# Graph attention on one core: weight loads on ScalarE's queue, residual rows in eight loads, other places for two steps, and a new order of the last two tiles

## The reference

```python
n, d = x.shape                      # 2048, 256
h = Wq.shape[1] // d                # 8
q = (x @ Wq).reshape(h, n, d)
k = (x @ Wk).reshape(h, n, d)
v = (x @ Wv).reshape(h, n, d)
a = jnp.einsum('hnd,hmd->hnm', q, k) * d ** (-0.5)
a = a + adj + adj
mask = adj == 0.0
a = jnp.where(mask, -1000000.0, a)
a = jax.nn.softmax(a, axis=-1)
a = jnp.where(mask, 0.0, a)
out = jnp.einsum('hnm,hmd->hnd', a, v)
out = out.transpose(1, 0, 2).reshape(n, h * d)
x = layernorm(x + out @ Wout)       # over the last axis, eps 1e-05
```

## Time and profile before

| | |
|---|---|
| median of 3 runs | 1853.81 us (1853.4 to 1855.88) |
| the profiled execution | 1851.97 us |
| its span in the trace | 1850.2 us |
| TensorE busy (matmul) | 1808.3 us, 98% |
| VectorE, ScalarE, GpSimd busy | 1117.0, 851.5, 983.8 us |
| moved by the 16 DMA engines | 345.96 MB, 187 GB/s on average |

### The profile page before, as it was taken

The page is one execution under the profiler, slowest core; times in us unless marked ns, Lnnn a source line. Parts: engine busy times, 40 slices in busy tenths (PEclk is TensorE's granted clock), DMA queues, the critical chain, the costliest instruction groups (busy, mean ns, idle before and its releaser), DMA issues.

```text
span 1850.2 us, 29363 instructions
## 1 busy us (share of the span) xinstructions
PE 1808.3 (98%) x10272; PEld 1580.0 (85%) x10272; DVE 1117.0 (60%) x2316; ACT 851.5 (46%) x1411; POOL 983.8 (53%) x764
## 2 busy tenths in 40 slices
PE   7989899999999999999999999999999999999997
PEld 6978788888898888988889888888888888898886
DVE  6788855555555555555655555555555556556667
ACT  4645554344554444544454444544454444554442
POOL 6787765444644446444564445634455444544443
PEclk9999999999999999999999999999999999999999
DMA  7787765666656666566664666656665566655664
GB/s 229 226 283 238 249 211 156 177 191 186 195 147 187 191 195 182 150 185 186 199 187 143 194 185 190 181 157 194 189 187 168 160 197 196 189 166 155 180 180 116
DMA packets 186962, 345.96 MB, mean 187 GB/s; under 512 B 39360, under 2 KB 96704, under 8 KB 170432
## 3 DMA queue, kind: packets, MB, share of 16 engines
q1 hardware_dynamic: 146112, 193.06, 37.2%
q10 hardware_dynamic: 40704, 151.03, 25.5%
HBM read 190.84 MB, written 18.87 MB: 113 GB/s over the span
## 4 chain that ended last, share of the span: by engine, by line
PE 87%; DVE 3%; issue 1%; SPq 1%; DMA 0%; POOL 0%; ACT 0%; DVEq 0%; ACTq 0%
PE bank L409 34%; PE y_bank L432 22%; PE bank L374 17%; PE y_bank L430 12%; PE y_bank L428 1%; SPq L306 1%; DVE blocks L653 1%; DVE zero_mark L691 0%; DVE y_acc L743 0%; POOL p_split L480 0%; DVE t_p L630 0%; DVE m_sb L697 0%; DMA raw_x<-in_x_dram 0%; PE bank L394 0%; ACT m_sb L560 0%
## 5 line engine op out<-in xcount | busy, mean ns | idle before, releaser
L480 POOL TENSOR_TENSOR p_split<-p_turned,p_split 128x512 fp32r<-128x512 f32 x512 | 651.5, 1301 | 628.7 <-ACT p_split L541 628.1
L409 PE MATMUL bank<-k_split,q_split 128*128 128x512 f32 x3072 | 790.0, 392 | 0.0
L432 PE MATMUL y_bank<-v_split,p_split 128*128 128x512 f32 x1920 | 701.8, 399 | 0.0
L409 PEld LDWEIGHTS bank<-k_split,q_split 128*128 128x128 f32 x3072 | 577.4, 188 | 110.5 <-issue 0.3
L630 DVE CUSTOM_DVE_ANT_0 t_p<-bank,m_sb 128x512 f32<-128x512 f32 x512 | 351.2, 687 | 339.9 <-PE bank L409 317.5
L430 PE MATMUL y_bank<-v_split,p_split 128*128 128x256 f32 x2048 | 555.7, 282 | 0.0
L532 ACT ACTIVATE t_p<-t_p,small 128x2048 f32<-128x2048 f32 x128 | 256.8, 2006 | 442.3 <-DVE small L642 442.3
L432 PEld LDWEIGHTS y_bank<-v_split,p_split 128*128 128x128 f32 x1920 | 362.7, 189 | 76.1
L430 PEld LDWEIGHTS y_bank<-v_split,p_split 128*128 128x128 f32 x2048 | 389.1, 190 | 18.7
L541 ACT ACTIVATE p_split<-p_turned 128x512 fp32r<-128x512 f32 x512 | 291.9, 620 | 167.1 <-DMA p_turned<-blocks 166.9
L653 DVE STREAM_TRANSPOSE blocks<-t_p 128x2048 f32<-128x2048 f32 x128 | 295.9, 2312 | 106.3 <-ACT t_p L532 74.1
(11 more groups left out here) (45 smaller groups left out, 716.3 us busy)
## 6 DMA issues: line engine op xcount, KB each, us to landing
m_sb<-m_dram ACTq DMA_DIRECT2D x112, 1024.0 KB, 5.4
p_turned<-blocks SPq DMA_DIRECT2D x1536, 64.0 KB, 2.2
p_turned<-blocks ACTq DMA_DIRECT2D x512, 64.0 KB, 2.3
raw_w<-in_L_gnn_Wk_dram SPq DMA_DIRECT2D x64, 256.0 KB, 3.8
blocks<-in_adj_dram SPq DMA_DIRECT2D x64, 256.0 KB, 4.4
raw_w<-in_L_gnn_Wq_dram SPq DMA_DIRECT2D x64, 256.0 KB, 3.7
m_dram<-m_sb SPq DMA_DIRECT2D x16, 1024.0 KB, 6.6
raw_w<-in_L_gnn_Wv_dram SPq DMA_DIRECT2D x64, 256.0 KB, 3.8
```

What stands on the lines that cost most here:

```text
L409: mm = nc.tensor.matmul(dst[:], q[:, a, k, f * P:(f + 1) * P], k_split[:, kk, k, b * BANK:(b + 1) * BANK], start=(i == 0), stop=(i == len( ...
L432: mm = nc.tensor.matmul(y[:], hi, v_split[:, j].rearrange("p s d -> p (s d)"), start=False, stop=last)
L480: nc.gpsimd.tensor_tensor(lo, p_turned[:, i * BANK:(i + 1) * BANK].rearrange("p (j b) -> p j b", b=QUAD), hi.bitcast(F32), ALU.subtract).t ...
```

## The change

Six edits:

- Weights: `load_w` moves from SP's program to ScalarE's, behind the `hi_of` of the projection whose slot it refills. At the start weight 0 is given by ScalarE, weights 1 to 4 by SP between the adj loads; weights 5 to 9 follow the first five projections on ScalarE.
- Residual rows: instead of two loads at tau 2 and two at tau 6 (512 KB each) there are eight of 256 KB, one in each odd tau of head 0; `add_y` waits for each pair of tiles.
- The turn of the next head's x moves from (13, 1) to (13, 3).
- Output weight: it is loaded ahead of the adj loads of tile 1, and in tau 0 it is split behind bank 1 instead of behind bank 3.
- The last two tiles: in tau 126 and 127 all four banks of scores come ahead of the values.
- For these two tiles, SP shuffles two quadrants and ScalarE two (before three and one).

```diff
@@ due
-                if (t, b) == (TURN_X, 1):
+                if (t, b) == (TURN_X, 3):
                     yield "x", h + 1
@@ numbers
-        Y_LATE = TILES // 2
+        W_FROM = {"k": wk, "q": wq, "vt": wv}
+        LAST_TILES = ALL - 2
@@ helpers
+        def w_columns(n):
+            kind, _, c = w_keys[n]
+            return W_FROM[kind].rearrange("(k p) n -> p k n", p=P)[:, :, c * D:(c + 1) * D]
...
+        def moved_by_sync(tau):
+
+            return QUADS - 1 if tau < LAST_TILES else QUADS // 2
@@ block.sync
-                loaded = [0]
-
-                def load_w(upto):
-                    while loaded[0] < min(upto, len(w_keys)):
-                        n = loaded[0]
-                        loaded[0] = n + 1
-                        key = w_keys[n]
-                        if n >= SLOTS:
-                            sp.wait_ge(projected, nth[w_keys[n - SLOTS]] + 1)
-                        columns = src[key[0]].rearrange("(k p) n -> p k n", p=P)[:, :, key[2] * D:(key[2] + 1) * D]
-                        sp.dma_start(raw_slot[n % SLOTS][:], columns).then_inc(w_loaded[n % SLOTS], 16)
+                def load_w(n):
+                    sp.dma_start(raw_slot[n % SLOTS][:], w_columns(n)).then_inc(w_loaded[n % SLOTS], 16)
...
-                def load_y(c_first, c_stop, loaded_sem):
-                    for f in range(HALVES):
-                        sp.dma_start(y_tokens[:, f, c_first:c_stop], x_tokens[f][:, c_first:c_stop]
-                                     ).then_inc(loaded_sem, 16)
+                def load_y(c):
+                    if c >= 2:
+                        sp.wait_ge(y_loaded[c % 2], 16 * (c // 2))
+                    sp.dma_start(y_acc[:, c * HALVES:(c + 1) * HALVES], x_pairs[c]).then_inc(y_loaded[c % 2], 16)
...
-                    for j in range(QUADS - 1):
+                    for j in range(moved_by_sync(tau)):
...
                 load_x(0)
+                load_w(1)
+                load_adj(0, 0)
                 load_w(2)
-                load_adj(0, 0)
+                load_w(3)
+                load_adj(0, 1)
                 load_w(4)
-                load_adj(0, 1)
-                load_w(5)
                 load_adj(0, 2)
                 load_adj(0, 3)
-                load_w(SLOTS + 2)
+                load_wout(0)
                 for q in range(BANKS):
                     load_adj(1, q)
-                load_w(SLOTS + len(START))
-                load_wout(0)
                 for tau in range(ALL + 1):
...
                         load_adj(t + 2, 0)
-                    if tau == 2:
-                        load_y(0, Y_LATE // 2, y_early)
-                    if tau == 6:
-                        load_y(Y_LATE // 2, C, y_late)
+                        if t % 2:
+                            load_y(t // 2)
                     for i in range(QUADS):
-                        if tau < ALL:
-                            load_w(w_by[tau, i] + SLOTS)
@@ block.tensor
-                        if tau >= LAG:
+                        if LAG <= tau < LAST_TILES or tau >= ALL:
+                            values(tau - LAG, g)
+                    if LAST_TILES <= tau < ALL:
+                        for g in range(BANKS):
                             values(tau - LAG, g)
@@ block.gpsimd
-                    if t == 0 and tau < ALL:
-                        lo_wout(tau // TILES)
+                        if t == 0 and tau < ALL and b == (1 if tau == 0 else BANKS - 1):
+                            lo_wout(tau // TILES)
@@ block.scalar
+                def load_w(n):
+                    if n < len(w_keys):
+                        if n >= SLOTS:
+                            act.wait_ge(projected, nth[w_keys[n - SLOTS]] + 1)
+                        act.dma_start(raw_slot[n % SLOTS][:], w_columns(n)).then_inc(w_loaded[n % SLOTS], 16)
...
-                    j = QUADS - 1
-                    act.dma_start(p_turned[quad(j), i * BANK:(i + 1) * BANK],
-                                  turned_place(tau)[quad(i), j * BANK:(j + 1) * BANK]).then_inc(shuffled[i], 16)
-
+                    for j in range(moved_by_sync(tau), QUADS):
+                        act.dma_start(p_turned[quad(j), i * BANK:(i + 1) * BANK],
+                                      turned_place(tau)[quad(i), j * BANK:(j + 1) * BANK]).then_inc(shuffled[i], 16)
+
+                load_w(0)
                 hi_w(1)
...
                 for key in START:
                     hi_of(key)
+                    load_w(w_order[key] + SLOTS)
                     hi_w(w_order[key] + 4)
...
                             hi_of(key)
                             if key in w_order:
+                                load_w(w_order[key] + SLOTS)
                                 hi_w(w_order[key] + 3)
...
-                    if t == 0 and tau < ALL:
-                        hi_wout(h)
+                        if t == 0 and tau < ALL and b == (1 if tau == 0 else BANKS - 1):
+                            hi_wout(h)
@@ block.vector
-                    if tau == 0:
-                        dve.wait_ge(y_early, 32)
-                    if tau == Y_LATE:
-                        dve.wait_ge(y_late, 32)
+                    if tau < TILES and t % HALVES == 0:
+                        dve.wait_ge(y_loaded[t // HALVES % 2], 16 * (t // HALVES // 2 + 1))
```

More of the change, by code:

```diff
@@ L119, in graph_attention_layernorm @@
         wout_loaded, wout_hi, wout_lo = sem("wout_loaded"), sem("wout_hi"), sem("wout_lo")
-        y_early, y_late = sem("y_early"), sem("y_late")
+        y_loaded = [sem(f"y_loaded{i}") for i in range(2)]
         projected, proj_hi = sem("projected"), sem("proj_hi")
@@ L138, in graph_attention_layernorm @@
         adj_rows = adj.rearrange("(f p c) j -> c f p j", f=HALVES, c=C)
-        x_tokens = x.rearrange("(f p c) e -> f p c e", f=HALVES, c=C)
+        x_pairs = x.rearrange("(f p c) e -> c p f e", f=HALVES, c=C)
         out_tokens = out.rearrange("(f p c) e -> f p c e", f=HALVES, c=C)
@@ L198, in graph_attention_layernorm @@
             in_order(key)
-        w_by = {}
         for tau in range(ALL):
@@ L204, in graph_attention_layernorm @@
                     in_order(key)
-                w_by[tau, b] = len(w_order)
         w_keys = list(w_order)
-        Y_LATE = TILES // 2
+        W_FROM = {"k": wk, "q": wq, "vt": wv}
+        LAST_TILES = ALL - 2
         EARLY_NORM = TILES - 3
@@ L249, in _ @@
             def _(sp):
-                src = {"k": wk, "q": wq, "vt": wv}
                 def load_x(h):
@@ L342, in _ @@
                         load_wout(h + 1)
-                assert loaded[0] == len(w_keys)
                 def store_out(first, stop):
```

## The result

The changed kernel takes 1841.3 us (median of 4 runs, 1840.46 to 1842.29) against 1854.85 us (4 runs on the same chip): ratio 0.9922, 95% interval 0.9908 to 0.9936. Predicted were 1840, between 1832 and 1848. A later set of four runs of the same kernel gave 1842.35 us and 0.9936 (0.9922 to 0.9950). The profiled execution has the highest of the four times (1842.29); its span is 1840.6. Against the profiled execution before that is 9.7 us less (1851.97 - 1842.29 = 9.68).

The account below looks back on a forecast made before the run. TensorE, busy 98% of the span, bounds the kernel, but VectorE's chain paces head 0 from tile 2. Terms -5.5 - 3.6 - 4.9 - 0.5 + 1.0 + 1.2 = -12.3 from 1851.97 give 1839.7, say 1840 us; range 1832 to 1848.

Parts of the forecast that it names:

- The start, -5.5: At the start, TensorE's waits for the late k weight and the output weight go: 5.5 us saved, bounds 0 and 7.25.
- the 1842.8: Sum if, by the skill's rule alone, the start gave back only five issues of 0.47 us: 2.4 us, not 5.5.
- The residual rows, -3.6 and -4.9: In head 0, spreading the loads removes VectorE's idle before the transposes of tiles 2 and 6: 8.5 us saved.
- part is given back: Rival, 13%: VectorE's pace swallows half the residual rows' gain and exp is 0.6 us late in six tiles: about 1848.
- the 13.5: Sign of being wrong: tile spacing over 13.5 us in odd tiles of head 0, from ScalarE's issues.
- Weights off SP in head 0, -0.5: In head 0, q weights' issues of 0.58 us leave SP's shuffles: 0.5 us saved, range -3.5 to +3.6.
- The turn of x, +1.0: Turning the next head's x later makes VectorE wait for ScalarE's high half: 1.0 us lost, bounds 0 and 1.9.
- the turn to head 1, 0: At the turn to head 1, TensorE's 3.7 us of waits keep their distance from VectorE's chain: no gain.
- The end, +1.2: At the end, eight shuffle issues on ScalarE instead of four delay root and end by 1.25 us; bounds -3.9, +2.
- More freed: Rival, 13%: all 7.25 at the start, 8.5 from residual rows, 2 from SP's issues, 1.5 at the end: 1833.
- The slower case: Rival, 7%: weights behind mask loads on ScalarE's queue land after 9.2 us, holding TensorE in heads 1 to 7: 1862.

Follow-up runs that it names:

- e5: The changed kernel with all weights loaded by SP again and the start's loads in their old order: 1849.22 us, ratio 0.9972.
- e6: The changed kernel with the output weight loaded behind the adj loads of tile 1 and split at the end of tile 0 again: 1845.2 us.
- e7: The changed kernel with the first weight given by SP behind x instead of by ScalarE at the same time: 1841.04 us.
- e3: The changed kernel with the residual rows loaded in two bursts of two 512 KB loads at tau 2 and 6 again: 1848.03 us.
- e9: The changed kernel with GpSimd's adds to the mask cut to 128 x 8 elements, leaving most of the mask without those values: 1839.39 us.
- e4: The changed kernel with the next head's x turned two banks earlier again, at bank 1 instead of bank 3: 1842.1 us.
- e1: The changed kernel with SP giving twelve of sixteen shuffles and ScalarE four for the last two tiles, as before the change: 1840.22 us.

## Why the prediction was right, step by step

**The start, -5.5.** Right, in size and in cause: 5.6 at tile 1. e5 brings back the late weight (3.05 us of wait), e6 the 2.40. It was an order in SP's queue, not a transfer at its limit. The total alone couldn't tell: the 1842.8 that the prediction works out with 2.4 us for the start lies 1.5 from the median, and 1840 lies 1.3 from it. The post of tile 1 tells. The rule that several issuers save only issue time (the Trainium skill, "DMA: Bandwidth & Descriptors", section "Issuing engines are not separate DMA queues") has no room for it: 2.4 us by that alone, and e6's output weight, which stays on the same queue and is only loaded and split earlier, is worth more. Of bandwidth it holds: x lands at 4.4 to 4.9 us in the nine profiles that give the first weight beside it, and at 3.5 to 3.8 in the five that give it behind, a small cost that the prediction put at nothing and that comes to nothing (e7).

**The residual rows, -3.6 and -4.9.** The mechanism was right (e3: back to 1848), the terms too large: 3.1 and 2.5 by the posts. The waits went entirely, as predicted, but the four tiles from 2 to 6 took 52.75 us, and not the 50.35 that are left of 55.25 without the wait of 4.90. It is no accident of one profile: the twelve with spread loads have 51.9 to 53.7. So 2.4 us were given back, the rival "part is given back" in small. My first reading, that VectorE was stretched by GpSimd (its busy time in these tiles went from 45.50 to 48.16 us), named a true effect and not the cause: e9 brings it down to 45.81, and the tiles still take 52.5. Nor are all of the 2.4 us the price of spreading: e3, with its burst, takes 51.6 for them without its wait of 5.28. What the spread loads do show is the step from tile 4 to 5, 13.0 us and more against 12.7 and 12.8. It passes the 13.5 that the prediction named as a sign of being wrong (13.8 in the changed kernel); but ScalarE's issues of weights, which it named as the reason, are not it, since e5 without them has 13.9. A likely account of the rest is that two chains of nearly the same length pace head 0, VectorE's own work and the shuffle from `blocks[0]`, so that cutting one uncovers the other; no run isolates it, and the cause stays open.

**Weights off SP in head 0, -0.5.** Nothing between tiles 6 and 13 as far as it can be read. But the step looked at the wrong place: it counted issues of 0.58 us and heads 1 to 7, not the turn, where weights that must wait for their slots hold the shuffle's transfers behind them on SP's queue. Undoing this edit costs 4.2 us from tile 13 to 20 (e5), far more than the term; the waits of VectorE before the three transposes there, 5 to 6.5 us each in e5, are 1.78, 0.72 and 0.77 in the changed kernel. These waits are mostly covered, though: the kernel before has them too (6.03, 5.85 and 5.62 us), and it takes only 1.1 us longer than the changed one over these tiles.

**The turn of x, +1.0, and the turn to head 1, 0.** The wait of VectorE for the high half of x came (0.78 us), and cost nothing (e4). The turn to head 1 gave 1.1 and not 0. The 4.2 us that e5 loses there are more than that, and e5 differs from the kernel before at this place in the turn of x, which is late in it. Whether late x and weights on SP are worse together than each alone wasn't tried.

**The end, +1.2.** Here the step failed in size: +2.4. Counted from the start of the last transpose, the root is 1.44 us later (7.66 instead of 6.22), near the 1.25 worked out. "The normalisations, not the last product, hold the last adds up" was a right reading of the kernel before: its last product ends at 19.4, and the last sum is added at 20.8 without a wait. In the changed kernel it holds only for the sum before the last, which is added at 18.4 us instead of 17.0. The last add waits 0.93 us for TensorE. TensorE begins the last sum at 14.8 instead of 13.4, behind the splits that stand behind the root, and takes 8.3 us for it instead of 5.9, as its clock is at half for most of it. So the last add comes at 23.2 instead of 20.8, 2.4 later: 1.4 as worked out, and 1.0 of a lower clock that the prediction didn't have and that the normalisations don't cover.

**The rivals.** More freed: the residual rows gave 5.6 us and not 8.5, and the end took time instead of giving it. The slower case, weights late behind mask loads: refuted, TensorE waits nowhere from 300 to 1810 us, and the page of the profile has medians of 3.4 to 3.9 us to landing for weights and 5.2 for masks. Between the profiled executions the sum is 2.6 us too large, 12.3 for 9.7: 1.4 up to the turn to head 1 and 1.2 at the end. Within the 1.4 the misses partly cancel: 2.9 too much for the residual rows and 0.8 too much for tiles 6 to 13, against 1.0 for x and 1.1 for the turn that came better than forecast. That 1840 lies within 1.3 us of the median all the same is partly luck in which execution was profiled, at 1851.97 us below all four times before the change, and at 1842.29 the highest of the four after it.

## What to carry to other kernels

Before moving transfers between queues, look for a transfer on the queue that must wait for a slot, and count what stands behind it: here the waits, not the issues of 0.6 us, were worth 2.6 us in the start and 4.2 at the turn of the head when the weights went back to SP's queue (e5). When idle time before an instruction goes, don't count on all of it: of the 4.90 us before one transpose here, 2.5 arrived, and a second chain of like length is the first thing to look for. Giving an engine more transfers to issue is paid by what stands behind them on that engine, and at the end of this kernel nothing covered it (e1).

## What the runs showed of the hardware

**An operation of VectorE can wait for one of GpSimd, and the wait is counted as busy.** The denominator's operation on 128 x 1 elements takes 0.21 us alone and up to 1.38. VectorE's rows and GpSimd's of the changed kernel:

```profile
140.02 0.49 DVE L661 SCALAR_TENSOR_TENSOR small<-small 128x1 f32<-128x1 f32 x1
...
166.01 1.09 DVE L661 SCALAR_TENSOR_TENSOR small<-small 128x1 f32<-128x1 f32 x1
```

```profile
137.95 3.80 POOL L472 TENSOR_TENSOR p_split<-p_turned,p_split 128x512 fp32r<-128x512 f32 x3
...
162.03 5.05 POOL L472 TENSOR_TENSOR p_split<-p_turned,p_split 128x512 fp32r<-128x512 f32 x4 [0.93 <-ACT p_split L539]
```

The second ends at 167.10 and GpSimd's fourth split at 167.09; the first ends at 140.51 and GpSimd's second of three at 140.50. VectorE's operation waits for the end of the split that is running, which here takes 1.25 to 1.3 us. The Trainium skill, "SBUF — State Buffer", section "SBUF: two separate sides", says that an operation of VectorE with two inputs in SBUF and one of GpSimd that reads SBUF exclude each other for the whole instruction; the traces agree, and e9 shows it by taking the partner away (1.21 us in all eleven).

**TensorE's clock after short waits.** In the changed kernel the granted clock fell to 0.50 (1.2 of 2.4 GHz) within the wait of 5.04 us at the turn to head 1, for 6.8 us (230.8 to 237.6), and within that of 4.11 us at the end, again for 6.8 us. The wait alone doesn't set the length: at the same place 4.10 and 4.36 us of wait brought 3.4 us at 0.50 in e4 and e5, as did 3.38 us in e1. The last sum of values takes 5.9 us at full clock (before the change), 7.3 to 7.5 with 3.4 us of the low one (e4, e5 and e1) and 8.3 in the changed kernel.
